# V in two copies, for even and odd heads, and the products of two heads added by TensorE

## The reference

```python
h = _layernorm(x, norm1_g, norm1_b)
qkv = h @ qkv_w + qkv_b                    # 16 heads of 16
scores = einsum('bld,blwd->blw', q, kw) / 4  # w: 15 neighbours of each token
out = einsum('blw,blwd->bld', softmax(scores), vw)
x = shortcut + out @ proj_w + proj_b
x = x + gelu(_layernorm(x, norm2_g, norm2_b) @ fc1_w + fc1_b) @ fc2_w + fc2_b
...
main = gelu(x @ W1m + b1m) @ W2m + b2m
logits = mean(x, axis=1) @ w_gate + b_gate  # top 2 of 8, softmax weights
expert_out = sum_k gate_w[k] * (gelu(x @ W1e[k] + b1e[k]) @ W2e[k] + b2e[k])
x + a * main + (1 - a) * expert_out
```

## Time and profile before

| | |
|---|---|
| median of 3 runs | 2017.33 us (2017.32 to 2019.91) |
| profiled execution | 2016.5 us, of which span 2014.7 us |
| PE busy | 1919.4 us (95%) |
| PE weight load busy | 1718.1 us (85%) |
| DVE busy | 1509.9 us (75%) |
| ACT busy | 1135.4 us (56%) |
| POOL busy | 866.5 us (43%) |
| mean granted clock of PE | 0.992 |

### The profile page before, as it was taken

One profiled execution on the slowest core, in us unless ns is written; L12 is line 12 of the kernel. 1 busy time (PEld: TensorE's weight loads), 2 busy tenths in 40 slices (PEclk: granted clock), 3 DMA queues, 4 the chain that ended last, 5 costly groups with the idle time before them and its releaser, 6 DMA issues.

```text
span 2014.7 us, 49639 instructions
## 1 busy us (share of the span) xinstructions
PE 1919.4 (95%) x19598; PEld 1718.1 (85%) x19598; DVE 1509.9 (75%) x2462; ACT 1135.4 (56%) x1801; POOL 866.5 (43%) x790
## 2 busy tenths in 40 slices
PE   6889999999999999999999999999999999999999
PEld 5778889898898988889888898888979888898898
DVE  8687786867868687786877868678696886868743
ACT  5565555656556555555655556455565655655554
POOL 5326344362534526335263443624336252453635
PEclk9999999999999999999999999999999999999999
DMA  4121210212112121110212102121021211212111
GB/s 122 32 64 53 59 49 28 74 48 74 44 35 63 42 74 54 46 56 27 75 54 56 52 26 74 51 74 39 28 69 48 74 44 39 63 38 75 43 57 54
DMA packets 188895, 109.57 MB, mean 54 GB/s; under 512 B 65436, under 2 KB 187640, under 8 KB 188664
## 3 DMA queue, kind: packets, MB, share of 16 engines
q1 hardware_dynamic: 187316, 105.43, 18.3%
q10 hardware_dynamic: 1348, 0.98, 0.2%
HBM read 85.52 MB, written 8.39 MB: 47 GB/s over the span
## 4 chain that ended last, share of the span: by engine, by line
PE 63%; DVE 27%; issue 6%; ACT 3%; POOL 1%; DMA 0%; DVEq 0%; SPq 0%; ACTq 0%; POOLq 0%
PE psB L235 35%; PE psA L235 23%; DVE hr_lo L535 5%; DVE smax L608 3%; DVE pr L612 3%; DVE pr L594 2%; DVE smax L601 2%; PE psA L993 2%; DVE qm L578 2%; DVE acc L712 2%; DVE tm L627 1%; PE psA L1092 1%; DVE tm L629 1%; PE psA L1114 1%; DVE acc L551 1%
## 5 line engine op out<-in xcount | busy, mean ns | idle before, releaser
L535 DVE TENSOR_TENSOR hr_lo<-hf,hr_hi 128x512 fp32r<-128x512 f32 x512 | 483.1, 944 | 407.1 <-ACT hr_hi L843 405.0
L843 ACT ACTIVATE hr_hi<-hf 128x512 fp32r<-128x512 f32 x512 | 323.8, 632 | 274.4 <-PE psB L235 186.0
L441 POOL TENSOR_SCALAR wx_hi<-raw 128x512 fp32r<-128x512 f32 x256 | 209.1, 817 | 623.7 <-PE psB L235 355.6
L443 POOL TENSOR_TENSOR wx_lo<-raw,wx_hi 128x512 fp32r<-128x512 f32 x256 | 401.8, 1569 | 21.4
L235 PE MATMUL psB<-wx_hi,hr_hi 128*128 128x256 f32 x1024 | 287.4, 281 | 0.2
L235 PE MATMUL psB<-wx_hi,hr_lo 128*128 128x256 f32 x1024 | 286.3, 280 | 0.0
L235 PE MATMUL psB<-wx_lo,hr_hi 128*128 128x256 f32 x1024 | 285.8, 279 | 0.0
L839 ACT ACTIVATE hf<-psB,b1x 128x512 f32<-128x512 f32 x256 | 174.9, 683 | 186.8 <-PE psB L235 170.8
L235 PE MATMUL psB<-z_hi,wx_hi 128*128 128x512 f32 x512 | 211.8, 414 | 0.0
L235 PE MATMUL psB<-z_hi,wx_lo 128*128 128x512 f32 x512 | 202.3, 395 | 0.0
L235 PEld LDWEIGHTS psB<-wx_hi,hr_hi 128*128 128x128 f32 x1024 | 192.5, 188 | 10.6 <-DVE hr_lo L535 0.9
(11 more groups left out here) (155 smaller groups left out, 4819.5 us busy)
## 6 DMA issues: line engine op xcount, KB each, us to landing
raw<-in_L_ffn_W1e SPq DMA_DIRECT2D x256, 128.0 KB, 2.2
raw<-in_L_ffn_W2e SPq DMA_DIRECT2D x256, 128.0 KB, 2.2
out_x<-acc SPq DMA_DIRECT2D x32, 256.0 KB, 2.2
xin<-in_L_attn_x SPq DMA_DIRECT2D x15, 512.0 KB, 3.7
vb<-vs SPq DMA_DIRECT2D x64, 96.0 KB
vb<-vs SPq DMA_DIRECT2D x62, 80.0 KB
tm<-in_L_ffn_b2e SPq DMA_DIRECT2D x32, 128.0 KB, 3.0
raw<-in_L_attn_fc_w SPq DMA_DIRECT2D x8, 256.0 KB, 4.7
```

Of the source, the lines that this page charges most:

```text
L441: g.tensor_scalar(wx[0][:, s, :], raw[:, s, :], 1.0, 0.0, ALU.mult, ALU.add).then_inc(w_hi.sem, 1)
L443: g.tensor_tensor(wx[1][:, s, :], raw[:, s, :], wx[0][:, s, :].bitcast(f32), ALU.subtract).then_inc(w_lo.sem, 1)
L535: v.tensor_tensor(hr[1][:, c % 2, :], hf[:, c % 3, :], hr[0][:, c % 2, :].bitcast(f32), ALU.subtract).then_inc(h_lo.sem, 1)
L843: a.activation(hr[0][:, c % 2, :], hf[:, c % 3, :], ACT.Copy).then_inc(h_hi.sem, 1)
```

## The change

V's windows are kept twice: vs and vb get an index p of two. In copy 0 the odd heads' features are zero, in copy 1 the even heads'. DVE writes each copy's heads in values, one instruction for each copy (runs of 16 features); the zeros are written once, at the start. attend now runs, for each block, over both p: the copy p by the 32 columns of pT that are that head's queries, the second added to the first in PSUM. What comes out has no wrong half: for each group of 64 features, units 0 and 1 (then 2 and 3) fill the 512 tokens of one PSUM bank side by side. So attended, emask and aT go. attended_high and attended_low read PSUM, for one group of 64 partitions at a time. PE no longer waits for DVE between units, but for attended_low ahead of unit 2.

```diff
-                        for gr in range(G):
-                            keys = slice(GW * gr, GW * gr + KW)
-                            for n in range(2):
-                                to, cols = GW * gr + HP * n, slice(2 * QB * n, 2 * QB * n + 2 * QB)
-                                last = pe.matmul(psA[to:to + HP, 2 + gr, 2 * QB * b:2 * QB * (b + 1)], vb[keys, j, 2 * th + h, c, HP * n:HP * n + HP],
-                                                 pT[keys, b, cols], start=True, stop=True)
+                        at = (th * UB + b) * QB
+                        for p in range(2):
+                            for gr in range(G):
+                                keys = slice(GW * gr, GW * gr + KW)
+                                for n in range(2):
+                                    to, col = GW * gr + HP * n, (2 * n + p) * QB
+                                    last = pe.matmul(psA[to:to + HP, 2 + gr, at:at + QB], vb[keys, j, 2 * th + h, p, c, HP * n:HP * n + HP],
+                                                     pT[keys, b, col:col + QB], start=p == 0, stop=p == 1)
...
             def attend(t, u):
-                if u:
-                    pe.wait_ge(aT_s.sem, aT_s.at(t, HS * u - 1))
-                else:
+                if u == 2:
+                    pe.wait_ge(tA_lo.sem, tA_lo.at(t, G - 1))
+                elif u == 0:
...
             def values(t, n):
-                v.wait_ge(tr1.sem, tr1.all(t))
-                v.tensor_tensor(vs[:, 2 * n:2 * n + 2, :], psA[:, 2 if n or t == 0 else 0, :].rearrange("p (i n) -> p i n", n=D),
-                                bv[:, :].unsqueeze(1).to_broadcast([P, 2, D]), ALU.add).then_inc(vs_s.sem, 1)
+                if t:
+                    v.wait_ge(vb_in.sem, vb_in.all(t - 1))
+                for p in range(2):
+                    dst, src, bias = (a.rearrange("p i (h e d) -> p i h e d", e=2, d=HD)[:, :, :, p, :] for a in (
+                        vs[:, 2 * n:2 * n + 2, p, :], psA[:, 2 if n or t == 0 else 0, :].rearrange("p (i n) -> p i n", n=D),
+                        bv[:, :].unsqueeze(1).to_broadcast([P, 2, D])))
+                    v.tensor_tensor(dst, src, bias, ALU.add).then_inc(vs_s.sem, 1)
...
             def attended_low(t, c):
-                v.wait_ge(tA_hi.sem, tA_hi.at(t, c))
-                v.tensor_tensor(zT[1][:, c, LEFT:LEFT + T], aT[:, c, :], zT[0][:, c, LEFT:LEFT + T].bitcast(f32), ALU.subtract).then_inc(tA_lo.sem, 1)
+                for gr in range(G):
+                    rows = slice(GW * gr, GW * gr + GW)
+                    v.wait_ge(tA_hi.sem, tA_hi.at(t, G * c + gr))
+                    v.tensor_tensor(zT[1][rows, c, LEFT:LEFT + T], psA[rows, 2 + gr, :], zT[0][rows, c, LEFT:LEFT + T].bitcast(f32), ALU.subtract
+                                    ).then_inc(tA_lo.sem, 1)
...
-                    elif q == 2 and f >= 0:
+                    elif q == 6 and f >= 0:
                         route_bias(f)
```

More of the change, by code:

```diff
@@ L95, in build @@
         qm = sb("qm", [P, 2, UB, HS * QB])
-        vs = sb("vs", [P, NT, D])
-        tn = vs
-        vb = sb("vb", [PK, HS, NT, KD, GW])
+        vs = sb("vs", [P, NT, 2, D])
+        vb = sb("vb", [PK, HS, NT, 2, KD, GW])
         pr = sb("pr", [P, 2, UB, G, GW])
+        tn = pr[:, 0, :, :, :].rearrange("p b g k -> p (b g k)").rearrange("p (i n) -> p i n", n=D)
         pT = sb("pT", [P, UB, P])
@@ L267, in windows @@
                 for gr in range(G):
-                    dst = vb[GW * gr + key:GW * gr + key + n, s, tiles[0]:tiles[-1] + 1, :, :]
-                    src = vs[at:at + n, tiles[0] - back:tiles[-1] + 1 - back, :].rearrange("p i (c g n) -> p i c g n", c=KD, g=G)[:, :, :, gr, :]
-                    eng.dma_start(dst.rearrange("p i c n -> p (i c) n"), src.rearrange("p i c n -> p (i c) n")).then_inc(vb_in.sem, 16)
+                    dst = vb[GW * gr + key:GW * gr + key + n, s, tiles[0]:tiles[-1] + 1, :, :, :]
+                    src = vs[at:at + n, tiles[0] - back:tiles[-1] + 1 - back, :, :].rearrange("p i e (c g n) -> p i e c g n", c=KD, g=G)[:, :, :, :, gr, :]
+                    eng.dma_start(dst.rearrange("p i e c n -> p (i e c) n"), src.rearrange("p i e c n -> p (i e c) n")).then_inc(vb_in.sem, 16)
         block = ctx.enter_context(nc.Block())
@@ L409, in _ @@
             roots(1, *EXTRA[1])
[L410 to L415, removed]
+            const(g.memset(hmask[:, :], 1.0))
+            for h in range(2):
+                v = hmask[64 * h:64 * h + 64, :]
+                const(g.affine_select(out=v, in_=v, compare_op=ALU.is_ge, fill=0.0, base=0, pattern=[[-HD, HS]], channel_multiplier=1))
+                const(g.affine_select(out=v, in_=v, compare_op=ALU.is_ge, fill=0.0, base=HD - 1, pattern=[[HD, HS]], channel_multiplier=-1))
             const(g.memset(band[:, :], 0.0))
@@ L593, in mask @@
                         v.wait_ge(trp.sem, trp.at(t - 1, 2 * (u + 2) + 1))
+                    if u == 0:
+                        v.wait_ge(tr1.sem, tr1.all(t))
                     v.scalar_tensor_tensor(
@@ L679, in norm1_z @@
                 v.wait_ge(rstd[0].sem, rstd[0].at(row - 1))
-                v.wait_ge(vb_in.sem, vb_in.all(row - 1))
+                v.wait_ge(trp.sem, trp.all(row - 1))
                 for i in range(NT):
@@ L764, in _ @@
                         shift(t, 2)
-                    elif q == 6 and t < ROWS:
-                        attended(t, 0)
                     elif q == 7 and t < ROWS:
@@ L769, in _ @@
                         shift(t, 3)
-                    elif q == 8 and t < ROWS:
-                        attended(t, 1)
                     elif q == 9 and t < ROWS:
@@ L775, in _ @@
                         normalise(t, 3)
-                    elif q == 11 and t < ROWS:
-                        attended(t, 2)
                     elif q == 12 and t < ROWS:
-                        attended(t, 3)
                         attended_low(t, 1)
@@ L907, in attended_high @@
                     a.wait_ge(val.sem, val.all(t))
-                a.activation(zT[0][:, c, LEFT:LEFT + T], aT[:, c, :], ACT.Copy).then_inc(tA_hi.sem, 1)
+                for gr in range(G):
+                    rows = slice(GW * gr, GW * gr + GW)
+                    a.activation(zT[0][rows, c, LEFT:LEFT + T], psA[rows, 2 + gr, :], ACT.Copy).then_inc(tA_hi.sem, 1)
             table(ACT.Gelu_apprx_tanh)
@@ L1119, in project @@
                 pe.wait_ge(tA_lo.sem, tA_lo.all(t))
-                pe.wait_ge(aT_s.sem, aT_s.all(t))
                 for h in range(2):
```

39 lines of the change are left out of this document (11 added, 28 removed).

## The result

The changed kernel takes 1986.42 us, the median of 4 runs (1984.88 to 1988.34), against 2018.62 us for the kernel before beside it. The ratio is 0.984, 95% interval 0.982 to 0.986. The forecast was 1967 with a range of 1945 to 1999: the direction and the range hold, the mechanism in part, and the gain is 31 us where 50 were forecast (against the 2017 us of the kernel before that the forecast started from; 32 against the runs beside it). The profiled span went from 2014.7 to 1983.5 us. I compare the two traces in the order of the rows shown before.

The account below looks back on a forecast made before the run. PE, busy 1919 of 2015 us, bounds the kernel; its waits for DVE ahead of turn and scores 2 total 72.0 us. 15 x 3.0 + 2 (start) + 3 (clock) = 50 off 2016.5: 1966.5, so 1967; range 1945 to 1999.

Parts of the forecast that it names:

- The waits: PE's gaps ahead of turn 0, scores 2, turn 2 and turn 3, 4.81 us in the row read, would mostly go.
- So both waits go, 3.16 us: With route_bias out of slot 2, PE's waits ahead of turn 0 (1.88 us) and scores 2 (1.28 us) vanish.
- A unit of attend: On PE, twice the matmuls of half the columns would cost 0.12 us more a unit, 1.0 us from 0.88.
- The 29 ns a place: In attend, 32 moving columns take 29 ns at each of four places, so the columns bound the unit: 0.93 us.
- The clock: With PE's waits gone, some of about 16 us lost to the lower granted clock returns: 3 us, bounds 0 and 13.
- Row 0: At the start, PE's 1.78 us ahead of the first scores goes, windows take some back: 2 us gained, bounds -1 and +6.
- So I leave the issue at 9.2: SP's issuing of V's windows stays at 9.2 us, since an issue doesn't follow the bytes it moves.
- route_bias off the path: On DVE, route_bias moves from slot 2 to slot 6, where POOL is quiet, and takes 3.7 us, not 4.43.
- values under 1 us: On DVE, the two instructions of values that write V's copies would take under 1 us together.
- the second rival: In attend, the second copy's matmul waits for the first at the same PSUM place: 2.4 us a unit, 2035 us; chance 0.07.
- The first rival: A floor in each attend matmul: a unit takes 1.86 us, a row gains only 0.8, 2003 us; chance 0.10.
- The third: DVE late again at turn 2 and 3, with route_bias at 4.43 and attended_low at 2.5: 1988 us; chance 0.20.

Follow-up runs that it names:

- The hold: The changed kernel, with POOL's third and fourth weight split of a row made only once DVE has written qm for unit 2: 1968.07 us, ratio 0.976.

## Why the forecast had the sign right and the size wrong

Between scores 2 of row 1 and of row 15, fourteen rows, PE's start times give 122.8 us a row before and 120.7 after: 29.2 us of the 31.2 in the span. The forecast for the same stretch was 45 (14 x 3.0, and 3 for the clock). To compare term by term, its numbers are put as the trace has them, gaps and work apart. Of the 4.81 us of gaps in its row it left 1.1 (0.4 ahead of turn 2 and 0.7 ahead of turn 3), 3.7 less, or 3.5 in the mean row. Four units of attend, each 0.12 longer, take back 0.5. That leaves its 3.0.

- **The waits.** Forecast 3.5 a row less, measured 2.2 (61.0 us of gaps became 30.2): 18 us short. The step that failed is "So both waits go, 3.16 us. It is close: DVE is ready only 0.1 us before PE". Turn 0 went as worked out. Ahead of scores 2, 19.1 us are left in these rows. The forecast noted that normalise was stretched, but gave slot 4's h_low its quiet 0.7 without placing POOL's fourth split beside it. In the row that it read this split ended at 492.15, a quarter of a microsecond ahead of h_low's new place at 492.4:

```profile
490.88 1.27 POOL L443 TENSOR_TENSOR wx_lo<-raw,wx_hi 128x512 fp32r<-128x512 f32 x1
```

  In the changed kernel the split comes 0.7 us later, counted from scores 1 of the row, and lasts 1.87. h_low falls on it and takes 1.78. The hold removes the collision and with it the wait. With the hold this stretch has 13.4 us of gaps, 0.96 a row, where the forecast had 1.1 left: with POOL out of the way its working comes out.
- **A unit of attend.** Forecast +0.12, measured +0.22, 1.03 to 1.25: 0.87 a row in place of 0.5, 5 us short. The 29 ns a place went by columns, and a place takes 35. The forecast also let the units ahead of turn 2 and 3 vanish in waits, which they do only as long as DVE is what PE waits for. Now DVE waits for PE at the gather, so turn 2 and 3 move with PE:

```profile
509.52 1.45 DVE L549 SCALAR_TENSOR_TENSOR acc<-psB,al,acc 128x512 f32<-128x512 f32 x2 [1.57 <-PE psB L233]
```

- **The clock.** Forecast 3 us back, and these rows gave 10. They had 23.9 us at the lower level and now have 3.4; at half the clock that is 11.9 and 1.7 us lost. It is also what the other terms leave (29.2 - 30.8 of gaps + 12.2 of attend = 10.6). This offsets a third of the two shortfalls, and that is luck: the forecast took 3.
- **Row 0.** Forecast 2 us less; the second row's first scores start 2.5 later, 106.08 for 103.54. The 1.8 ahead of the first scores went (they start at 17.78 for 19.20), but the windows landed 6.7 us after PE wanted them, and 13.7 us at the lower clock began in that wait. "So I leave the issue at 9.2" failed: the issues took 12.9 in a steady row and doubled in row 0. In the steady rows the slack was large enough for that; in row 0 it was not.
- **What held.** route_bias off the path (2.2 rather than 3.7, better than taken), attended_high at 1.19, values under 1 us, and no stall between the two copies' products: the second rival would have shown in a unit of 2.4. attended_low takes 1.40 for its pair although it runs beside a split. Before, with both inputs from SBUF, it took 1.78 beside the same split (L633 at 519.95).

```profile
514.22 1.40 DVE L622 TENSOR_TENSOR zT_lo<-psA,zT_hi 64x512 fp32r<-64x512 f32 x2
```

```profile
513.84 1.61 POOL L441 TENSOR_TENSOR wx_lo<-raw,wx_hi 128x512 fp32r<-128x512 f32 x1
```

The first rival, a floor in each matmul, was right as a mechanism and wrong in its size (1.12 us from first to last start, not 1.86). The third, DVE late again, was right that DVE would be late, but at scores 2 and not at turn 2 and 3.

What stays open: why the clock kept its upper level in nearly all steady rows though gaps of 1.5 us remained; why POOL's splits come later against PE in the changed kernel; and whether row 0's wait can be hidden altogether. Larger pieces took some of it off: 5.2 to 5.8 us in three profiles, where the small ones show 6.4 to 7.2.

## What to carry to other kernels

When a change moves an engine's work earlier, list what runs on the other engines at the new time, and price each moved instruction for that neighbour, not from its old row. A quiet duration and one beside a POOL instruction differed here by a factor of 2.6, and two held splits were worth nearly as much as the whole change. Two edits that each lift one of two successive limits must be timed together: apart these gave -3 and +7 us, together -31. Before halving the columns of a tiled matmul, check the floor: at four places, 64 to 32 moving columns saved 36% of the time for each product, not 50%, and 32 to 16 saved 1 to 3% for either operand alone.

## What the runs showed that I had not expected

In a single wait of 6.7 us early in the program the granted clock fell, and it stayed at the 1.2 GHz level for 13.7 us, which costs up to 7 us. SP's issues of the same eight copies took 6.05, 10.60 and 12.12 us with more bytes and then more pieces, so an issue is not free of what it moves. And the order of two groups of DMAs on SP changed the time by 53 us. PE never waited for the chunks themselves, and for the windows 6.2 us with the chunks first and 5.8 with the windows first; the 53 come by way of when POOL gets its data.
